# Sampling stage of a four-layer convolution kernel: two TensorE passes per convolution in place of five, two PSUM banks per step, hats for four steps at once

## The reference, cut to what matters

```
xr   = conv1x1(x, w_reduce, b_reduce)              # 192 -> 180 channels
offs = conv1x1(xr, w_offset, b_offset)             # 360 channels: 2 x 180
f_w  = deform_conv2d(xr, offs[:, :180], w_dcnw, b_dcnw)
f_h  = deform_conv2d(xr, offs[:, 180:], w_dcnh, b_dcnh)
f    = attn0 * f_h + attn1 * f_w                   # softmax over the image means
out  = conv1x1(f, w_expand, b_expand)
```

## Time and profile before

| what | us |
|---|---|
| median of three runs | 12080.69 |
| profiled execution, its own time | 12053.83 |
| its span, first to last instruction | 12051.9 |
| sampling stage, first to last sampling matmul (632 to 7218 of the span) | 6586 |
| the same, per tile of 20 steps | 45.73 |

### The profile page before, as it was taken

How to read it: one execution, slowest core, us unless ns; L and a number is a source line. 1 busy time by engine, 2 the same in 40 slices (tenths; PEclk the granted TensorE clock), 3 DMA queues, 4 the chain that set the end, 5 groups by cost and what they waited for, 6 DMA issues and landing times. The chain is left out here.

```text
span 12051.9 us, 337397 instructions
## 1 busy us (share of the span) xinstructions
PE 11074.3 (92%) x133078; PEld 8457.9 (70%) x133078; DVE 9815.6 (81%) x14111; ACT 10353.3 (86%) x10426; POOL 5059.6 (42%) x3633
## 2 busy tenths in 40 slices
PE   6689999999999999999999999850899899999999
PEld 4389999999999999999999984420633455555555
DVE  4578888888888888888888886799878788888888
ACT  3299999999999999999999993596778899998998
POOL 0033333333333433343333430133200588888887
PEclk9899999999999999999999995985999899999999
DMA  6488888888888888888888888444544333333332
GB/s 165 129 223 213 214 218 217 218 214 211 215 214 214 217 216 219 218 219 216 215 216 215 219 205 198 136 163 132 171 150 156 116 101 102 108 101 103 101 101 85
DMA packets 818421, 2128.02 MB, mean 177 GB/s; under 512 B 145699, under 2 KB 414369, under 8 KB 674497
## 3 DMA queue, kind: packets, MB, share of 16 engines
q1 hardware_dynamic: 800912, 2072.13, 64.3%
q10 hardware_dynamic: 15120, 30.71, 0.7%
q0 software_dynamic: 832, 3.59, 0.1%
HBM read 1782.85 MB, written 323.30 MB: 175 GB/s over the span
## 5 line engine op out<-in xcount | busy, mean ns | idle before, releaser
L884 PE MATMUL dc_p<-dc_t 96*64 96x90 f32 (+1 forms) x103896 | 4658.9, 247 | 144.9 <-issue 71.7
L884 PEld LDWEIGHTS dc_p<-dc_t 96*64 96x64 f32 x103896 | 4370.8, 136 | 418.1 <-issue 416.4
L955 POOL TENSOR_TENSOR dc_t<-dc_t 128x324 f32<-128x324 f32 (+1 forms) x2885 | 2591.8, 898 | 4028.3 <-DVEq L1043 2738.2
L1019 DVE TENSOR_TENSOR dc_t<-dc_p,dc_t 128x810 f32<-128x810 f32 (+1 forms) x2886 | 3043.5, 1055 | 896.4 <-DVEq L1016 861.1
L831 ACT ACTIVATE dc_t<-dc_t 96x2304 f32<-96x2304 f32 x1447 | 3189.0, 2204 | 105.6 <-ACTq L830 104.5
L836 ACT ACTIVATE dc_t<-dc_t 96x2304 f32<-96x2304 f32 x1446 | 3049.9, 2109 | 0.0
L2545 DVE TENSOR_TENSOR_SCAN ms_t<-ms_t,ms_p 128x512 f32<-128x512 f32 x1728 | 2127.0, 1270 | 283.7 <-PE ms_p L2487 203.7
L2461 POOL TENSOR_TENSOR ms_t<-ms_t 128x1536 f32<-128x1536 f32 x576 | 1987.9, 3456 | 503.3 <-DVE ms_t L2545 499.6
L2497 PE MATMUL ms_p<-ms_t,top_t 128*128 128x512 f32 x3456 | 1774.7, 596 | 0.0
L925 PE MATMUL dc_p<-dc_t 128*128 128x180 f32 (+1 forms) x7488 | 1536.5, 337 | 3.4 <-issue 2.0
L2487 PEld LDWEIGHTS ms_p<-top_t,ms_t 128*128 128x128 f32 x6912 | 850.9, 141 | 966.4 <-issue 693.8
(11 more groups left out here) (258 smaller groups left out, 9527.7 us busy)
## 6 DMA issues: line engine op xcount, KB each, us to landing
dc_t<-sxd SPq DMA_DIRECT2D x1447, 864.0 KB, 6.1
ms_t<-bcd SPq DMA_DIRECT2D x576, 256.0 KB, 3.3
dc_t<-xrT SPq DMA_DIRECT2D x49, 675.0 KB, 9.7
kvd<-wk_t SPq DMA_DIRECT2D x18, 1536.0 KB, 5.1
szd<-mi_t SPq DMA_DIRECT2D x36, 768.0 KB, 4.4
xvd<-mi_t SPq DMA_DIRECT2D x36, 768.0 KB, 4.8
dld<-mi_t SPq DMA_DIRECT2D x36, 768.0 KB, 3.4
ms_t<-dld SPq DMA_DIRECT2D x36, 768.0 KB, 6.8
```

The lines of the kernel that those rows point to most:

```text
L884: ins = e.matmul(PT[j % 2][o:o + 64, t // 3, t % 3 * nr * CG:(t % 3 + 1) * nr * CG], HX[:, m // 2 % RP, m % 2, t * 128 + o:t * 128 + o + 6 ...
L955: e.tensor_tensor(ZH[:, n % 4, :, 0:m], z[:, :, 0:m], z[:, :, nr * CG - m:nr * CG], ALU.add)\
L1019: e.tensor_tensor(Zt[:, n % 4, 0:nr * LEN].rearrange("p (b m i) -> p b m i", b=3, i=CG), PT[n % 2][:, :, 0:3 * nr * CG].rearrange("p b (m ...
```

## The change

Nothing outside `sample_and_convolve` changes. The parts:

1. TensorE handles a convolution in two passes, `passes = [(0, 4, range(5)), (4, 6, range(5, 13))]`: four steps with 5 blocks, then six steps with 8 blocks. `LEAD` goes from 6 to 10 steps. `PR` and `PF` get two banks each (the two convolutions' sums lie in separate banks of `PF`).
2. The slots of the ring are given back at the first contraction matmul of a pass: 2 after the first, 3 after the second. `RP` stays 8.
3. ACT's `distance` and `hats` work on two slots at once (96 x 4608); the loop issues distance(r+1), which waits for both of its loads, ahead of hats(r).
4. A step's result lies in two banks. With 5 rows: 25 (tap, row) groups in the first bank and 20 in the second, 25 weighed in each (the rest zeroed once). With 6 rows: 27 in each, for which tap 4 is cut into two matmuls of 3 rows.
5. DVE copies a pass out in one copy; `rows` comes in two halves; weigh runs 10 and 11 steps ahead and quarter 8. `halve` on POOL runs 9 ahead.
6. SP issues the sums' load after load q = 4 and the stores after q = 9.

```diff
-    RP, AHEAD, LEAD = 8, 12, 6
-    EXTRA = AHEAD // 2 + 1
+    RP, AHEAD, LEAD = 8, 12, 10
+    EXTRA = AHEAD // 2 + 2
...
+    passes = [(0, 4, range(5)), (4, 6, range(5, NCK))]
...
+        def spread(nr):
+            if nr == 5:
+                return [(t, 0, 5, t // 5, t % 5 * 5) for t in range(TAPS)]
+            return [(t, 0, 6, 0, 6 * t) for t in range(4)] + [(4, 0, 3, 0, 24), (4, 3, 3, 1, 0)] + \
+                [(t, 0, 6, 1, 6 * t - 27) for t in range(5, TAPS)]
...
-                            if q == 3:
+                            if q == 4:
+                                sum_load(i, 2 + b * NT + y)
+                            if q == 9:
...
+                def distance(r):
+
+                    o = 2 * r % RP
+                    e.wait_ge(s_bx[o], 16).then_inc(s_bx[o], -16)
+                    e.wait_ge(s_bx[o + 1], 16).then_inc(s_bx[o + 1], -16)
+                    e.activation(HX[:, o:o + 2, :, :], HX[:, o:o + 2, :, :], ACT.Abs, bias=QX[:, 0:1]).then_inc(s_ab, 1)
...
-                    for n in range(NBB):
+                    for n in range(0, NBB, 4):
                         i, j = n // NB, n % NB
-                        if n % 2 == 0:
-                            distance((n + AHEAD) // 2 + 1)
-                            hats((n + AHEAD) // 2)
-                        if j in (4, 5, 9, 10):
-                            row_weights((i + 1) % NRB, (4, 5, 9, 10).index(j))
+                        distance((n + AHEAD) // 4 + 1)
+                        if j in (4, 8):
+                            row_weights((i + 1) % NRB, j // 2 - 2)
+                        hats((n + AHEAD) // 4)
+                        if j in (4, 8):
+                            row_weights((i + 1) % NRB, j // 2 - 1)
...
+                    for n in range(0, NBB, NG):
+                        i, conv = n // NB, n // NG % 2
+                        for first, count, blocks in passes:
+                            e.wait_ge(s_va, count).then_inc(s_va, -count)
+                            for u, c in enumerate(blocks):
+                                ins = e.transpose(PR[:, u // 4, u % 4 * 128:(u % 4 + 1) * 128],
+                                                  VA[:, conv, 128 * c:128 * (c + 1)], k.ident[:, :])
+                            if first == 0:
+                                ins = turn_sum((i - 1) % NRB, conv)
+                            ins.then_inc(s_tr, 1)
+                            for m in range(n + first + LEAD, n + first + LEAD + count):
+                                e.wait_ge(s_pt, 1).then_inc(s_pt, -1)
+                                sample(m % NBB)
+                            e.wait_ge(s_vt, 1).then_inc(s_vt, -1)
+                            if first == 0:
+                                e.wait_ge(s_ff, 1).then_inc(s_ff, -1)
+                            for u, c in enumerate(blocks):
+                                o = min(128, NG * LEN - 128 * c)
+                                ins = e.matmul(PF[:, conv, 0:CM], VT[0:o, u, :], WD[0:o, c, conv, :],
+                                               start=(c == 0), stop=(c == NCK - 1), skip_group_check=True)
+                                if u == 0:
+                                    ins.then_inc(s_free, count // 2)
...
                     for n in range(0, NBB, 2):
-                        unload(n)
-                        if n % NB in (2, 4, 6, 8):
-                            rows((n // NB + 1) % NRB, n % NB // 2 - 1)
-                        weigh(n + 6)
-                        quarter(n + 4)
-                        weigh(n + 7)
-                        sum_rows(n + 4)
-                        if n % NG == NG - 2:
-                            add_up(b, n // NB, n // NG % 2)
+                        i, j, conv = n // NB, n % NB, n // NG % 2
+                        for first, count, blocks in passes:
+                            if j % NG == first:
+                                unload(i, conv, first, blocks)
+                        if j == NG:
+                            add_up(b, i, 0)
+                        if j < 4:
+                            rows((i + 1) % NRB, j // 2)
+                        weigh(n + 10)
+                        quarter(n + 8)
+                        weigh(n + 11)
+                        sum_rows(n + 8)
+                        if j == NB - 2:
+                            add_up(b, i, 1)
```

More of the change, by code:

```diff
@@ L733, in sample_and_convolve @@
         QX = p.sb([W, 1])
-        PT = [p.ps([128, 3, 512]) for _ in range(2)]
-        PR = p.ps([128, 512])
-        PF = p.ps([128, 512])
+        PT = [p.ps([128, 2, 512]) for _ in range(2)]
+        PR = p.ps([128, 2, 512])
+        PF = p.ps([128, 2, 512])
         (s_w, s_hy, s_ab, s_hx, s_t, s_z, s_va, s_tr, s_vt, s_free, s_f, s_ff, s_out, s_fin, s_rw, s_hyf, s_pt, s_va2,
@@ L817, in _ @@
                 e.wait_ge(s_sb, 16).then_inc(s_sb, -16)
-                e.wait_ge(s_free, RP + 2 - EXTRA).then_inc(s_free, EXTRA - 2 - RP)
+                e.wait_ge(s_free, RP + LEAD // 2 - EXTRA).then_inc(s_free, EXTRA - RP - LEAD // 2)
                 store_tile(0, B * NT, s_fin)
@@ L826, in _, with hats @@
                 e.wait_ge(s_qx, 16).then_inc(s_qx, -16)
[L828 to L833, removed]
+                def distance(r):
[3 more added lines that the diff above has]
+                    e.activation(HX[:, o:o + 2, :, :], HX[:, o:o + 2, :, :], ACT.Abs, bias=QX[:, 0:1]).then_inc(s_ab, 1)
+                def hats(r):
+                    o = 2 * r % RP
                     e.wait_ge(s_ab, 1).then_inc(s_ab, -1)
-                    e.activation(HX[:, q % RP, :, :], HX[:, q % RP, :, :], ACT.Relu, bias=1.0, scale=-1.0)\
-                        .then_inc(s_hx, 2)
+                    e.activation(HX[:, o:o + 2, :, :], HX[:, o:o + 2, :, :], ACT.Relu, bias=1.0, scale=-1.0)\
+                        .then_inc(s_hx, 4)
                 def row_weights(i, step):
@@ L900, in _ @@
                     e.wait_ge(s_pt, 1).then_inc(s_pt, -1)
-                    if m % 2:
-                        e.sem_inc(s_free, 1)
+                    if m in (5, 9):
+                        e.sem_inc(s_free, 2)
                     sample(m)
+                e.wait_ge(s_pt, 2)
+                e.sem_inc(s_free, 1)
                 e.wait_ge(s_w, 16).then_inc(s_w, -16)
                 def body(b, y2, w):
[L907 to L924, removed]
-                            ins = e.matmul(PF[:, conv * CM:(conv + 1) * CM], VT[0:o, n // 2 % 2, u, :],
-                                           WD[0:o, c, conv, :], start=(c == 0), stop=(c == NCK - 1),
-                                           skip_group_check=True)
-                            if u == 0:
-                                ins.then_inc(s_free, 1)
-                        if g == NPR - 1:
-                            ins.then_inc(s_f, 1)
@@ L933, in _ @@
                 loops(e, body)
-                e.wait_ge(s_ff, 1).then_inc(s_ff, -1)
-                turn_sum(NRB - 1, 1).then_inc(s_tr, 1)
+                e.wait_ge(s_ff, 2).then_inc(s_ff, -2)
+                for conv in range(2):
+                    turn_sum(NRB - 1, conv, conv).then_inc(s_tr, 1)
                 e.wait_ge(s_hx, AHEAD - LEAD).then_inc(s_hx, LEAD - AHEAD)
-                e.wait_ge(s_va, 2).then_inc(s_va, -2)
+                e.wait_ge(s_va, LEAD - 4).then_inc(s_va, 4 - LEAD)
@@ L959, in body @@
                     for n in range(NBB):
-                        halve(n + 5)
-                for n in range(5):
+                        halve(n + 9)
+                for n in range(9):
                     halve(n)
@@ L968, in _ @@
             def _(e):
-                e.sem_inc(s_hyf, 2)
-                e.sem_inc(s_ff, 1)
+                e.sem_inc(s_ff, 2)
+                for q in range(2):
+                    e.memset(PT[q][:, 1, 360:512], 0.0).then_inc(s_ps, 1)
                 e.memset(ACC[:, 1:3, :, :], 0.0)
-                e.memset(FT[:, :, :, :], 0.0).then_inc(s_out, 3)
+                e.memset(VA[:, :, NG * LEN:NCK * 128], 0.0)
+                e.memset(HY[:, :, 5 * CM:5 * CM + 5], 0.0).then_inc(s_hyf, 2)
+                e.memset(FT[:, :, :, :], 0.0).then_inc(s_out, 2)
                 def rows(i, s):
@@ L1071, in _ @@
                 sum_rows(2)
+                weigh(6)
+                quarter(4)
+                weigh(7)
+                sum_rows(4)
+                weigh(8)
+                quarter(6)
+                weigh(9)
+                sum_rows(6)
                 loops(e, body)
-                e.wait_ge(s_tr, 1).then_inc(s_tr, -1)
-                keep_sum(1, 1)
+                for conv in range(2):
+                    e.wait_ge(s_tr, 1).then_inc(s_tr, -1)
+                    keep_sum(1, conv, conv)
                 e.wait_ge(s_half, 1).then_inc(s_half, -1)
                 e.wait_ge(s_sum, 1).then_inc(s_sum, -1)
-                e.wait_ge(s_hy, 1).then_inc(s_hy, -1)
 def mix_and_expand(nc, k):
```

78 lines of the change are left out of this document (37 added, 41 removed).

## The result

The changed kernel takes 13790.14 us (median of 4 runs, 13781.95 to 13803.13) against 12083.95 us for the kernel before beside it: a ratio of 1.141, 95% interval 1.139 to 1.143. It is 1706 us slower; the forecast was 1160 slower and 13240 us. The median lies 10 us under the upper end of the range, and the slowest of the four runs above it.

A forecast was written before the change was run, and what follows sets the result against it. The way from a freed ring slot to a usable one was taken as the bound: 51.7 us per tile plus 1.9 for the clock is 53.6, over 144.5 tiles 7745 us of stage, 13240 us in all; range 12200 to 13800.

The forecast's parts named there:

- The ring's way: From freed slots through loads, distance and hats to the next pass's end: 24.5 or 25.4 us; as bound, chance 0.76.
- the fall of the clock: TensorE drops to 1.2 GHz after idling before samples: one fall per tile on the path, 1.9 us.
- the chunk: A 675 KB load between the first and second load of a burst, once per three tiles: 2.9 us more.
- The sum: Sampling stage: 144.5 tiles at 53.6 us make 7745 us against 6586, so +1159 us.
- the added instructions of tap 4: TensorE in six-row tiles: cutting tap 4 in two adds 133 ns per step, 2.7 us per six-row tile.
- the 52 to 54 us: Sign that the prediction is right: the sampling stage takes 52 to 54 us per tile.
- waiting 343 us before its samples: TensorE in the kernel before: its waits before samples, set against ACT's 92 us and DVE's 770 us.
- the six pairs of lead: Ring of the kernel before: a pair waits only for a release six pairs back, 27 us.
- stay the bound: Rival: TensorE still sets the pace, 11970 to 12080 us; chance 0.12, of which 0.09 faster and 0.03 the same.
- fewer switches: TensorE between contraction, transposes and samples: five groups become two, saving 0.5 us per convolution, 1.0 per tile.
- the DVE rival: DVE sets the pace inside a pass, 3.1 us per pair against TensorE's 2.94: 12260 us; chance 0.06.
- The clock as a rival of its own: All three gaps of a tile leave TensorE at 1.2 GHz, 60.5 us per tile: 14240 us; chance 0.06.

The follow-up runs named there:

- e4: Changed kernel with ACT issuing hats(r) ahead of distance(r+1), bulk release and joined hats kept: 13170 us, ratio 1.090.
- e5: Changed kernel with a ring of ten slots in place of eight, nothing else: 13154 us, ratio 1.089.
- e10: Changed kernel with ten slots, given back one by one, each two pairs late: 12199 us, ratio 1.012.
- e3: Changed kernel with slots given back one by one and distance and hats on one slot at a time: 12199 us, ratio 1.0096.

## Why the prediction was right, and where it was not

**The ring's way.** Right in its place and nearly in its size. From the end of one pass of six to the next, the median of some 48 intervals at each of six places (three tiles of two convolutions) is 26.6 to 28.5 us where no chunk stands in the burst and 33.5 where one does. The prediction's terms give 25.4, 24.5 + 1.9 = 26.4 with the fall of the clock, and 26.4 + 2.9 + 1.6 = 30.9 with the chunk and two six-row pairs. TensorE idles where it was said: 3.1 and 3.6 us on average (6.1 behind a chunk) before the second pair of the pass of six in odd convolutions, where 3.6 was forecast, and 1.5 to 2.4 before its first in even ones, where it was about 2. Joined Abs and Relu take 4.04 and 3.93 us from start to start, as computed. Without a chunk the second load of a burst lands 10.3 us after the pass (10.1), the third 14.9 (13.8).

**The sum.** 53.6 us per tile were forecast and 57.7 measured. TensorE's own work is 44.3 - 0.4 = 43.9: the added instructions of tap 4 cost 80 ns per step (a six-row pair takes 3.64 us, 3.48 before), not 133, 0.5 per tile and not 0.9. The idle time is 9.1 us per tile where the terms had 51.7 - 44.3 = 7.4. What is left, 57.7 - 43.9 - 9.1 = 4.7 us, is put down to work at the lower clock (0.91 over the stage); the forecast had 1.9. The mis-sized term is thus the clock, with one fall per tile assumed and none in even convolutions, though the gaps of about 2 us there are nearly as long as those that cost 1.7 to 2.2 us in the earlier trace rows. The second error is 1.7 us of idle time. The mid-step stalls, of which the sum has no term, take 1.5 us per tile in this kernel. So the stage is outside the 52 to 54 us that the prediction asked for, and that the time is still in the range is by 10 us: in part luck.

**What the account didn't have.** It took the bulk release for a link of one way only, harmful because hats are joined and stand behind a wait. Take that link away alone and 620 us come back (e4 and e5 against the changed kernel). The next 955 us (e10 against e5) come back only when the loads are spread: stalls of TensorE inside steps, because its instructions are late behind a burst, and the slow clock behind them. The two prices don't add up to shares of the slowdown. In the changed kernel the ring's way stops TensorE first (7.5 of its 9.1 us of idle time stand before samples, 1.5 in mid-step), and the stalls grow to 4.1 us per tile once it is gone; the stalls alone taken away, with the way as it is, was not run. The chain of waits computed from single loads could not show them. The trace before did hold such stalls: all three idle times of the earlier trace rows (1.74 to 2.40 us, "issue") are in mid-step, and the prediction used them only for the clock.

**Two readings of the trace before.** The prediction has TensorE waiting 343 us before its samples. That row is of the weight loads (PEld); the idle time of the matmuls themselves is 94 us:

```profile
PE dc_p L884 <- issue: 65.5, 77, 2.5
PE dc_p L884 <- PEq L879: 28.8, 45, 2.8
```

TensorE leads all the more by that. And a slot of the kernel before is free one pair after its own samples, not at their end; the six pairs of lead are right, since the prediction's count has that pair in it.

**The rivals.** TensorE does not stay the bound in the changed kernel. With the releases spread it does (e3, e10), and then the change isn't worth its 1.0 us per tile of fewer switches: e3 is 1% slower than before, where 12040 us were expected. There the DVE rival's mechanism shows at TensorE, as some 0.3 to 0.5 us of idle time before most pairs that follow another without contraction between. In the rows of e3 below DVE's weigh (line 1030) ends at 3007.75, and the pair that needs its bank starts at 3008.18. Idle time is 1.8 us per tile in place of 0.7, and 0.5 go to tap 4; with 1.0 gained that makes 0.6 of the 0.9 us that e3 is over the kernel before, and the rest has no row. The clock as a rival of its own (14240) did not come: it cost about two and a half times as much as forecast (4.7 us per tile against 1.9), but not 2.9 us at every pair on the way.

```profile
3004.73 3.01 PE L892 MATMUL dc_p<-dc_t 96*64 96x90 f32 x72
3006.67 1.08 DVE L1030 TENSOR_TENSOR dc_t<-dc_p,dc_t 128x900 f32<-128x900 f32 x1
3008.18 3.03 PE L892 MATMUL dc_p<-dc_t 96*64 96x90 f32 x72 [0.44 <-PEq L887]
...
3017.04 3.02 PE L892 MATMUL dc_p<-dc_t 96*64 96x90 f32 x72 [0.29 <-PEq L887]
```

Line 892 is `sample`. Each pair in a pass stands behind a short wait that most pairs of the kernel before, with contraction between them, didn't have (0.7 us of idle time per tile in all). Not one run beat the kernel before.

## What to carry to other kernels

Give a ring's slots back one at a time, where the last reader of each is, even if the loop around them is coarser: here the same loads started in bursts of two and three cost 955 us on top of 12199. To find how tight a ring is, count from the release of a slot to the next use that needs it, with every engine's queue in order (a wait that stands ahead of finished work is a link), and compare with what the bound engine does in that time. And whoever puts idle time before TensorE's work should price the slow instructions behind it too: here they added about half as much as the idle time itself. Idle time in the middle of a group, where the program has no wait, is worth a look at the instruction packets in the DMA list.

## What the runs showed of the hardware

TensorE's instructions came in packets of 16.4 KB over the DMA engines that carry the data. In e4, with loads started in bursts, TensorE stopped 199 times in 6000 us for 1.0 to 3.5 us in the middle of a step, where the program has no wait, nearly once per convolution; 198 of these stalls ended 1.15 to 1.65 us after such a packet had landed, and they lay a multiple of 124 matmuls apart, one packet's worth. With the same loads spread, mid-step idle time fell from 486 us (e5) to 62 (e10) in 6000, with about as many packets per tile.

Four added fp32 matmuls per convolution, placed in idle time, made the kernel 163 us faster while the granted clock of the stage rose from 0.91 to 0.96.
